# A state-space layer whose every fifth product with B is formed on GpSimd, and whose convolution is three diagonal products on TensorE

## What is computed

```python
u = up_x @ W_up + b_up
left, right = jnp.split(u, 2, axis=-1)
xp = jnp.pad(left, ((0, 0), (K - 1, 0), (0, 0)))            # K = 3
conv = sum((conv_w[:, k] * xp[:, k:k + Lq, :] for k in range(K))) + conv_b
x = jax.nn.silu(conv)
delta = jax.nn.softplus(x @ W_delta + b_delta)
Bm = x @ W_B + b_B
Cm = x @ W_C + b_C
A = -jnp.exp(A_log)
dA = jnp.exp(delta[..., None] * A)
dBx = delta[..., None] * Bm[:, :, None, :] * x[..., None]
# over time: h = dA_t * h + dBx_t ; y_t = sum over the 64 states of h * C_t
y = y + D_skip * x
gated = y * jax.nn.silu(right)
return gated @ W_down + b_down
```

## Time and profile before

| | |
|---|---|
| median of 3 runs | 2139.44 us (2137.86 to 2139.44) |
| the profiled execution's own time | 2135.41 us |
| its span in the trace | 2133.6 us |
| TensorE busy / VectorE / ScalarE / GpSimd | 87% / 73% / 41% / 32% of the span |
| granted TensorE clock, mean | 0.968 of full |
| state-space layer: opening, first to last scan, ending | 1388 to 1425, 1427 to 1905, to about 1912 us of the trace |

### The profile page before, as it was taken

One profiled execution on the slowest core, in us unless ns is written; L12 is line 12 of the kernel. 1 busy time (PEld: TensorE's weight loads), 2 busy tenths in 40 slices (PEclk: granted clock), 3 DMA queues, 4 the chain that ended last, 5 costly groups with the idle time before them and its releaser, 6 DMA issues. The chain is left out here.

```text
span 2133.6 us, 23947 instructions
## 1 busy us (share of the span) xinstructions
PE 1862.2 (87%) x7515; PEld 996.0 (47%) x7527; DVE 1563.9 (73%) x2933; ACT 879.9 (41%) x2055; POOL 686.1 (32%) x757
## 2 busy tenths in 40 slices
PE   5779998999997999899888899968888878878998
PEld 2336653555553555567666455523232322225555
DVE  4868884555553788656556688749999999978887
ACT  2125544554543445345445333245444353332232
POOL 2642322433432222210110000027767677750000
PEclk8999999999999899999999899979999999999999
DMA  5000000000000000100000000000000000000000
GB/s 230 1 0 1 1 1 1 1 1 1 1 1 1 1 1 1 40 1 1 1 1 1 1 1 1 0 15 1 15 1 15 1 1 15 1 0 0 1 1 20
DMA packets 9628, 20.10 MB, mean 9 GB/s; under 512 B 1056, under 2 KB 8224, under 8 KB 8608
## 3 DMA queue, kind: packets, MB, share of 16 engines
q1 hardware_dynamic: 9504, 18.59, 2.6%
HBM read 14.39 MB, written 1.05 MB: 7 GB/s over the span
## 5 line engine op out<-in xcount | busy, mean ns | idle before, releaser
L1816 POOL TENSOR_TENSOR ssm_hc<-ssm_h,ssm_cm 128x512 f32<-128x512 f32 x256 | 334.3, 1308 | 135.3 <-DVE ssm_h L1899 135.0
L1899 DVE TENSOR_TENSOR_SCAN ssm_h<-banks,ssm_dbx 128x512 f32<-128x512 f32 x256 | 313.9, 1227 | 2.3 <-DVE ssm_dbx L1891 2.3
L515 PE MATMUL banks<-ffn_x_high,up_high 128*128 128x512 f32 x544 | 288.8, 531 | 6.0 <-ACT ffn_s1g L992 2.6
L1700 PE MATMUL banks<-ssm_hc,const 128*128 128x512 f32 x512 | 266.1, 601 | 12.2 <-DVE ssm_gated L1874 9.3
L1791 ACT ACTIVATE banks<-banks,a_neg 128x510 f32<-128x510 f32 x256 | 167.2, 659 | 242.6 <-PE banks L1687 241.6
L516 PE MATMUL banks<-ffn_x_low,up_high 128*128 128x512 f32 x544 | 218.3, 401 | 0.0
L517 PE MATMUL banks<-ffn_x_high,up_low 128*128 128x512 f32 x544 | 218.3, 401 | 0.0
L550 POOL TENSOR_TENSOR x_norm<-x_centred,x_square 128x512 f32<-128x512 f32 x28 | 37.9, 1354 | 492.5 <-ACT x_square L545 492.0
L1510 ACT ACTIVATE ffn_th<-banks 128x512 f32<-128x512 f32 (+1 forms) x136 | 81.2, 597 | 273.3 <-PE banks L517 224.6
L1891 DVE TENSOR_TENSOR ssm_dbx<-banks,ssm_bm 128x512 f32<-128x512 f32 x256 | 174.9, 683 | 19.3 <-PE banks L1690 18.8
L1325 POOL TENSOR_SCALAR wide_pin<-wide_pin,wide_rden 128x256 f32<-128x256 f32 x256 | 117.6, 478 | 217.0 <-DVE wide_rden L1349 217.0
(11 more groups left out here) (245 smaller groups left out, 3623.5 us busy)
## 6 DMA issues: line engine op xcount, KB each, us to landing
ssm_packed<-ssm_parts SPq DMA_DIRECT2D x48, 64.0 KB, 2.0
up_whole<-in_up SPq DMA_DIRECT2D x1, 2304.0 KB, 16.2
weights<-in_weights SPq DMA_DIRECT2D x1, 2048.0 KB, 21.4
up_whole<-in_up SPq DMA_DIRECT2D x1, 2048.0 KB, 7.9
const<-in_const SPq DMA_DIRECT2D x1, 1426.5 KB, 6.2
half<-in_half SPq DMA_DIRECT2D x1, 1408.0 KB, 9.7
weights<-in_weights SPq DMA_DIRECT2D x1, 1168.0 KB, 23.9
weights<-in_weights SPq DMA_DIRECT2D x1, 1152.0 KB, 11.2
```

The lines of the kernel that those rows point to most:

```text
L515: pe.matmul(out, w_high, x_high, start=True, stop=False)
L1700: pe.matmul(k.bank[5][:], k.c("hot")[:, P - row:2 * P - row], hc[:, i % HOLD, :], start=(i % NP == 0), stop=(i % NP == NP - 1)).then_inc(s ...
L1816: pool.tensor_tensor(hc[:, i % HOLD, :], h[:, i % HOLD, :], cm[:, i // NP % 2, :], ALU.mult) \
L1899: dve.tensor_tensor_scan(h[:, n % HOLD, :], k.bank[DELTA[n % AHEAD]][:], dbx[:, n % AHEAD, :], 0.0, ALU.mult, ALU.add).then_inc(s["h"], 1)
```

## The change

Two things change in `state_space`, and a few buffers share memory so that the new ones fit.

1. In each pass the steps 4, 9, 14, ... 59 (12 of 64, 48 in all; `by_pool`) get their product with B from GpSimd. GpSimd does not read PSUM here, so ScalarE first copies the bank to `dxs` (just ahead of the exponential of the step before), and GpSimd multiplies `dxs` with B into `pdbx` (behind its own product with C of four steps before). The scan of such a step reads `pdbx` in place of `dbx`. TensorE's two spreads of a step are parted: `spread_dx` runs one step earlier than `spread_delta` and waits for the use of its own bank.
2. The convolution's three taps leave VectorE. TensorE multiplies `left`, shifted by the tap, with a diagonal 128x128 matrix for each tap, at n = 19, ahead of the loop with `keep_clock` behind it; ScalarE takes half the sum and half the bias out of PSUM at n = 20, and VectorE makes `xs` in one instruction in place of two.

```diff
+    by_pool = lambda i: i % NP % 5 == 4
...
+                if n == 19:
+                    pe.wait_ge(s["right_in"], p + 1)
+                    pe.wait_ge(s["resets"], 1)
+                    for tap in range(3):
+                        ins = pe.matmul(two(k.bank[7]), w(f"conv{tap}"), left[:, :, tap:L + tap],
+                                        start=(tap == 0), stop=(tap == 2))
+                    ins.then_inc(s["conv"], 1)
...
+            def spread_dx(i):
...
+                if i >= AHEAD and by_pool(i - AHEAD):
+                    pe.wait_ge(s["dx_in"], pooled[i - AHEAD + 1])
+                elif i >= AHEAD:
+                    pe.wait_ge(s["dbx"], i - AHEAD + 1 - pooled[i - AHEAD + 1])
...
-                if n in (7, 10, 17, 27):
+                if n in (7, 10, 17, 19):
                     keep_clock(k, pe, WARM["first"])
...
+            spread_dx(0)
             for i in range(ALL + HOLD):
+                if i + 1 < ALL:
+                    spread_dx(i + 1)
                 if i < ALL:
-                    spread_rows(i)
+                    spread_delta(i)
...
+                if n == 20:
+                    act.wait_ge(s["conv"], p + 1)
+                    act.wait_ge(s["halved"], 1)
+                    act.activation(conv[:], k.bank[7][:], ACT.Identity, bias=half_b[:], scale=0.5).then_inc(s["conv_in"], 1)
...
             for i in range(ALL):
-                act.wait_ge(s["bc"], 2 * i + 1)
+                if i + 1 < ALL and by_pool(i + 1):
+                    m = pooled[i + 1]
+                    act.wait_ge(s["bx"], i + 2)
+                    if m >= 2:
+                        act.wait_ge(s["pdbx"], m - 1)
+                    act.activation(dxs[:, m % 2, :], k.bank[DELTA_X[(i + 1) % AHEAD]][:], ACT.Copy).then_inc(s["dx_in"], 1)
+                act.wait_ge(s["bc"], i + 1)
...
+                j = i + AHEAD + 1
+                if j < ALL and by_pool(j):
+                    m = pooled[j]
+                    pool.wait_ge(s["dx_in"], m + 1)
+                    pool.wait_ge(s["b_in"], j // NP + 1)
+                    if m >= 2:
+                        pool.wait_ge(s["h"], before[m - 2] + 1)
+                    pool.tensor_tensor(pdbx[:, m % 2, :], dxs[:, m % 2, :], bm[:, j // NP % 2, :], ALU.mult) \
+                        .then_inc(s["pdbx"], 1)
...
-                if n == 17:
-                    dve.wait_ge(s["left_in"], p + 1)
-                    link(dve.tensor_scalar(two(conv[:]), left[:, :, 0:L], taps[:, 0:1], w("conv_b"), ALU.mult, ALU.add))
-                if n == 18:
-                    link(dve.scalar_tensor_tensor(two(conv[:]), left[:, :, 1:L + 1], taps[:, 1:2], two(conv[:]),
-                                                  ALU.mult, ALU.add))
-                if n == 19:
-                    dve.scalar_tensor_tensor(two(conv[:]), left[:, :, 2:L + 2], taps[:, 2:3], two(conv[:]),
-                                             ALU.mult, ALU.add).then_inc(s["conv"], 1)
                 if n == 23:
                     dve.wait_ge(s["tanh_c"], p + 1)
-                    link(dve.scalar_tensor_tensor(conv[:], tc[:], 1.0, conv[:], ALU.add, ALU.mult))
-                if n == 24:
-                    dve.tensor_scalar(xs[:, p % 2, :], conv[:], 0.5, None, ALU.mult).then_inc(s["x"], 1)
+                    dve.scalar_tensor_tensor(xs[:, p % 2, :], tc, 1.0, conv[:], ALU.add, ALU.mult).then_inc(s["x"], 1)
...
-                if i < ALL:
-                    dve.wait_ge(s["bc"], 2 * i + 2)
+                if i < ALL and not by_pool(i):
+                    dve.wait_ge(s["bx"], i + 1)
```

More of the change, by code:

```diff
@@ L1606, in state_space @@
     ALL = PASSES * NP
-    s = k.semaphores("ssm", ["left", "left_in", "right", "right_in", "tanh_r", "conv", "tanh_c", "x", "delta", "z", "e", "u",
+    by_pool = lambda i: i % NP % 5 == 4
+    pooled = [0]
+    for i in range(ALL):
+        pooled.append(pooled[-1] + by_pool(i))
+    before = [i for i in range(ALL) if by_pool(i)]
+    s = k.semaphores("ssm", ["halved", "bx", "dx_in", "pdbx", "conv_in", "left", "left_in", "right", "right_in", "tanh_r", "conv", "tanh_c", "x", "delta", "z", "e", "u",
                              "ln", "b", "b_in", "c", "c_in", "gate", "ready", "rest", "split", "packed0", "packed1", "packed2", "packed3",
@@ L1614, in state_space @@
         left = sb("left", [P, NB, L + 2])
-        right, gate = sb("right", [P, T]), sb("gate", [P, 2, T])
-        conv, tc, xs = sb("conv", [P, T]), sb("tc", [P, T]), sb("xs", [P, 2, T])
+        rest = sb("rest", [P, 2, T])
+        right, tc = rest[:, 0, :], rest[:, 1, :]
+        gate = sb("gate", [P, 2, T])
+        conv, xs = sb("conv", [P, T]), sb("xs", [P, 2, T])
         z, e, u, ln, fix = (sb(name, [P, T]) for name in ("z", "e", "u", "ln", "fix"))
-        delta, dx, rest = sb("delta", [P, T]), sb("dx", [P, T]), sb("rest", [P, 2, T])
+        delta, dx = sb("delta", [P, T]), sb("dx", [P, T])
         parts = sb("parts", [P, 2, 3, T], BF16)
@@ L1637, in _ @@
                 if p >= 2:
[L1638 removed]
+                    sp.wait_ge(s["bc"], NP * (p - 1))
+                    sp.wait_ge(s["bx"], NP * (p - 1))
                 for g in range(4):
@@ L1831, in _ @@
             dve.wait_ge(s["resets"], 1)
-            taps = w("conv_w")
+            dve.tensor_scalar(half_b[:], w("conv_b"), 0.5, None, ALU.mult).then_inc(s["halved"], 1)
             def ahead(p, n):
@@ L2077 @@
     lay(5, "b_right", m["b_up"][P:, None])
-    lay(5, "conv_w", m["conv_w"])
+    for tap in range(3):
+        lay(5, f"conv{tap}", np.diag(m["conv_w"][:, tap]))
     lay(5, "conv_b", m["conv_b"][:, None])
```

43 lines of the change are left out of this document (24 added, 19 removed).

## The result

The changed kernel took 2149.96 us in the median of 5 runs (2148.02 to 2152.29), against 2139.44 (2135.83 to 2139.55) for the kernel before beside it: a ratio of 1.0053, 95% interval 1.0039 to 1.0068. It is slower by 10.5 us, 0.5%. The forecast was 2145, slower, with a range of 2122 to 2157.

What follows compares the result with a forecast made beforehand. VectorE, busy 114.1 of 117.9 us, was taken to bound the state-space layer. Savings of 28.1 and 7.2 us against added waits, blocking and opening summed to +6.1 us, making the median 2145 us, range 2122 to 2157.

Steps and rivals of the forecast that it cites:

- the opening carries the loss: Whole state-space stage: loop from first to last scan goes only from 477 to 478 us, so the loss sits ahead of it.
- Taken off VectorE, -35.3: VectorE's loop: 48 products with B save 28.1 us, and the taps, halving and a chained wait 7.2 us.
- Steps 41 to 49, +13.4: GpSimd and ScalarE in turn: later subtractions and copies delay scans 44, 45, 48 and 49, +4.5 us a pass.
- Steps 15 to 22, +11.9 and +2.8: TensorE's queue and table loads delay scans 16 to 22, +11.9 us; ScalarE's order at pass meetings delays step 16, +2.8.
- the norm comes 0.3 later through GpSimd's extra product: Around step 15: GpSimd's added product delays the norm by 0.3 us; scan 16 comes 0.2 late.
- Nothing behind step 22: Loop after the 2.3 us wait at step 22: no further late scan counted before step 44.
- Where passes meet, -0.9: Pass boundaries: step 8 is 1.4 us late in two passes, but the earlier spread shortens waits; -0.9 us in all.
- VectorE against GpSimd in SBUF, +8.7: Steps 23, 25, 32, 37: VectorE's pieces wait out running GpSimd products, 2.9 us a pass, +8.7 in all.
- The opening, +5: First pass ahead of the loop: diagonal products and ScalarE's work after them delay the first scan by 5 us.
- VectorE never waits for GpSimd's turn: Rival on SBUF sharing: all as forecast without the 8.7 us of blocking, giving 2136 to 2137 us; chance 0.2.
- the slack holds: Rival on loop waits: chains lengthen less than counted, giving 2109 to 2131 us; chance 0.15.
- GpSimd does not set the pace: Denies the rival that GpSimd's products, 1.38 us apart, limit the loop: 2159 us, range 2151 to 2165; chance 0.15.

Runs made afterwards that it cites:

- no_44_49: The changed kernel, but in the first three passes VectorE forms the products with B of steps 44 and 49 itself: 2142.65 us, ratio 1.0022.
- after: The changed kernel as made, with the whole change, against the kernel before: 2149.96 us, ratio 1.0053.
- no_14_24: The changed kernel, but in the first three passes VectorE forms the products with B of steps 14 and 24 itself: 2138.05 us, ratio 1.0001.
- opening: The changed kernel, but with the first pass's convolution on VectorE as in the kernel before: 2146.58 us, ratio 1.0033.
- late_24: The changed kernel, all work kept, with GpSimd's product for step 24 queued behind the product with C of step 21, not ahead: 2144.93 us, ratio 1.0030.
- no_24: The changed kernel, but in the first three passes VectorE forms the product with B of step 24 itself: 2146.34 us, ratio 1.0039.
- more: The changed kernel with convolution on VectorE and GpSimd's products only at steps 29, 52, 56, 60, and every fourth step of the last pass: 2114.39 us.

## Why the prediction was right, and where it was off

The side was right and the time lay 5 us under the measured one. Where the loss sits was wrong: "the opening carries the loss" gave the loop 1 us and the opening 5, and measured are 10 (7 by the medians) and 3.9. The waits in the loop grew by 34.2 and not by 27.2, the lengthened pieces came to 11 and not 8.7. That the side held has some luck in it: +6.1 was what was left of -35.3 and +41.4, and without the 8.7 for blocked pieces the sum would have been negative; the misses that follow nearly all made the kernel slower, so they could not turn it. The steps, in the order of the prediction:

- **Taken off VectorE, -35.3.** Right. Two scans stand 1.13 apart in front of the steps concerned, as the earlier trace rows had it, and the last pass, which pays for nothing, is 7.6 shorter: 12 times 0.58 and 0.7 at its start.
- **Steps 41 to 49, +13.4.** Right in mechanism and size. Forecast 1.2, 0.6, 1.0 and 2.6 at steps 44, 45, 48 and 49; measured 1.16, 0.61, 0.90 and 2.60 in each of three passes, and no_44_49 takes them away. The timeline of after shows the first two, to be read beside the earlier trace rows. GpSimd forms the product for step 44 at 1513.83 and so begins its first subtraction at 1516.28; ScalarE has waited 3.80 for it, and the scans of 44 and 45 wait 1.09 and 0.53:

```profile
1513.83 1.27 POOL L1863 TENSOR_TENSOR ssm_pdbx<-ssm_dxs,ssm_bm 128x512 f32<-128x512 f32 x1
...
1516.28 1.16 POOL L1843 TENSOR_TENSOR ssm_rest<-ssm_delta,ssm_parts 128x512 f32<-128x512 f32 x1
...
1517.47 0.63 ACT L1814 ACTIVATE ssm_parts<-ssm_rest 128x512 bf16<-128x512 f32 x1 [3.80 <-POOL ssm_rest L1843]
...
1518.73 1.23 DVE L1938 TENSOR_TENSOR_SCAN ssm_h<-banks,ssm_pdbx 128x512 f32<-128x512 f32 x1 [1.09 <-issue]
...
1521.07 1.22 DVE L1938 TENSOR_TENSOR_SCAN ssm_h<-banks,ssm_dbx 128x512 f32<-128x512 f32 x1 [0.53 <-DVE ssm_dbx L1926]
```

- **Steps 15 to 22, +11.9 and +2.8.** Right at 18 (0.9), 20 (1.4) and 22 (2.3). Wrong at 16, where 0.2 was forecast and another 1.4 in two passes: it is 1.6 in two passes and 2.4 in the third. The step that failed is "the norm comes 0.3 later through GpSimd's extra product". That took GpSimd's product for 14 at its length alone. It also waits 0.67 for its copy, and the norm's last product comes 1.65 later, counted from scan 12 (4.18 and not 2.53), in all three passes; in no_14_24 it is at 2.53 again. In the first, the norm's end (the product from 1456.37) and TensorE's product with the left half (1457.69, having waited 1.32) followed it:

```profile
1452.70 1.27 POOL L1863 TENSOR_TENSOR ssm_pdbx<-ssm_dxs,ssm_bm 128x512 f32<-128x512 f32 x1 [0.67 <-ACT ssm_dxs L1825]
...
1456.37 1.26 POOL L550 TENSOR_TENSOR x_norm<-x_centred,x_square 128x512 f32<-128x512 f32 x1
...
1457.69 1.13 PE L1674 MATMUL banks<-x_norm,weights 128*128 128x512 f32 x2 [1.32 <-POOL x_norm L550]
...
1459.07 0.69 DVE L1926 TENSOR_TENSOR ssm_dbx<-banks,ssm_bm 128x512 f32<-128x512 f32 x1 [1.11 <-PE banks L1715]
```

- **Nothing behind step 22.** Wrong, and the largest omission. The prediction followed ScalarE's table loads to the scan of 22 and stopped there; the copy for step 24 stands behind them too, and GpSimd's queue behind that copy. With the table loads late by the diagonal products this gave the gap at 28 (0.6 to 1.0), which in after, opening and no_44_49 comes only in passes in which the clock was low for 6.8 us from step 22 or 23 on, and it blocked the pieces of steps 23, 25 and 31. late_24 and no_24 show it: 8.8 and 8.4 us of the profiled loop, 5.0 and 3.6 by the medians. The profiled execution of after was its slowest, and single passes scatter by 2.9 us (in opening), so the medians are the better measure of what this is worth; against the kernel before in their own set they give 3.5 and 2.1.
- **Where passes meet, -0.9.** Off by some 2: at the three meetings the waits at steps 5 and 8 are 2.2 and 1.4, 1.5 and 0.6, 1.5 and none, and the first pass has 0.4 at its step 8, against about 2.2 at each meeting before.
- **VectorE against GpSimd in SBUF, +8.7.** The mechanism was right and the term too small: 11. The pieces of steps 23, 25, 32 and 37 are blocked as counted, by 0.4, 0.7, 1.1 and 0.5 us; not counted were that of step 31 (1.31 to 1.33 in place of 0.40), which has one input, and the gating product at the meetings (1.47 in place of 1.22). VectorE's timeline has both cases one step apart (the pieces of steps 36 and 37): at 1502.09 its piece starts 0.16 ahead of GpSimd's product and takes 0.66, and GpSimd's takes 1.63; at 1504.53 GpSimd's, started at 1503.84, runs, and VectorE's takes 1.13, ending 0.6 behind GpSimd's next start:

```profile
1502.09 0.66 DVE L1899 TENSOR_TENSOR ssm_fix<-ssm_ln,ssm_fix 128x512 f32<-128x512 f32 x1
...
1502.25 1.63 POOL L1853 TENSOR_TENSOR ssm_hc<-ssm_h,ssm_cm 128x512 f32<-128x512 f32 x1 [0.45 <-DVE ssm_h L1938]
...
1503.84 1.26 POOL L1863 TENSOR_TENSOR ssm_pdbx<-ssm_dxs,ssm_bm 128x512 f32<-128x512 f32 x1
1504.53 1.13 DVE L1901 SCALAR_TENSOR_TENSOR ssm_delta<-ssm_z,ssm_fix 128x512 f32<-128x512 f32 x1
```

  The Trainium skill (SBUF — State Buffer, Who interferes with whom) also lets one-input `tensor_scalar` instructions in VectorE's two-port mode take part in that lock. The trace agrees: 0.40 and 1.45 for the halving, 0.40 and 1.32 for the piece of step 31. The prediction used only the sentence on two inputs.
- **The opening, +5.** Right in mechanism; it is 3.9, and the kernel called opening gives 4.3 back. The six records of the diagonal products took 3.35 us, between the 2.6 and 5.2 of the two clock levels: the clock rose while they ran, at 1404.6. So +5 was the sum at mostly the low level.

```profile
1399.77 2.08 PE L1677 MATMUL banks<-x_norm,weights 128*128 128x512 f32 x2 [0.78 <-ACT ssm_left L1771]
...
1403.35 3.35 PE L1682 MATMUL banks<-ssm_left,weights 128*128 128x512 f32 x6
```

- **The rivals.** That VectorE never waits for GpSimd's turn fell with the pieces above. That the slack holds fell too: the waits went from 12.5 to 46.7. GpSimd does not set the pace: in the last pass it idles 0.45 in every five steps, and in more it keeps up at every fourth.

## What to carry to other kernels

Before work is moved to an engine with idle time, ask for each place where it goes what it will wait for there and what is ready behind it in that queue; three products that waited for a copy behind two table loads cost 3.5 to 5 us by the medians where they saved 1.7, and one position later in the queue they no longer held back the ready product behind them. Count the idle time of an engine only where no chain runs through it: here 28 products moved at quiet places, with the parted spread, gained 23 us over the kernel before, and 48 evenly spread ones with the parted spread and the convolution lost 10. When GpSimd gets fuller, look at every SBUF-only instruction of VectorE, those with one input included, and ask which of the two engines starts first.
